# GpSimd splits the expert weights beside the experts, and second attention's units stand in another order

## The chip, the cores and the metric

The kernel runs on one core of one Trainium2 chip. Its time is the device time of one execution in microseconds (us), as the median of three runs. A core has a matmul engine (TensorE, PE in the profile; PEld is its weight load), VectorE (DVE), ScalarE (ACT), GpSimd (POOL) and SyncE (SP, which here issues DMAs). Each takes its instructions in the order written, and semaphores make one engine wait for another. Of the names in the profile bank is PSUM, and arena, arena2, arena3, work, norms and w_raw are large SBUF areas that many tiles share one after the other.

## The reference, cut to what matters

```python
x = layernorm(x + attn(x, Wq, Wkv, Wo, bo))              # 16 sequences, 16 heads of 64
x = layernorm(x + xattn(x, ctx, ctx, igate, fgate, rms)) # mLSTM with decays, 4 heads
# the expert layer, within it:
xn = (x - mu) * rsqrt(var + eps) * gamma + beta
scores, idx = top_k(softmax(xn @ Wr + br), 2)            # 8 experts, 2 per token
full_e = relu(xn @ W1[e] + b1[e]) @ W2[e] + b2[e]        # W1: 256 x 1024, W2: 1024 x 256
c = relu(b1) @ W2 + b2
x = layernorm(x + sum_k scores_k * (full[idx_k] - c[idx_k] + sum_e c_e))
```

x is 16 sequences of 128 tokens of 256 numbers, all float32. A float32 matmul is done here as three passes in a rounded format (fp32r): each operand is split into hi, its rounded value, and lo, what is left, and hi*hi, hi*lo and lo*hi are added up in PSUM. So each weight has to be split once: a cast to hi, and a subtraction for lo. The 8 experts' weights are 4096 words per partition each, 8192 when split.

## The kernel before, in words

Tokens go through attention in 8 pairs of sequences. A pair i has four steps s = 0 to 3 (two halves of the heads by two sequences); with n = 4i + s, PE does in each step the scores of step n + 1 (L762), then a list of filler units, then the transposes of the softmax weights of step n (L793), a second list of fillers, and the weighted sums of step n (L805). The lists come from `fillers(i, s)`. They hold the projections of the next steps (q, k, v; three passes each, L664 to L666), the output projection (w), and the units of second attention and the router for earlier pairs: X and C (transposes of the layernormed input and of the context, L705), G (gates, L711 and L713), S (gate rows to columns, L720), T (scores of second attention, L726), U (its weighted sums, L735), N and L (transposes and logits for the router, L741 and L747). All units but w write one of two PSUM banks in turn, and a unit waits until its bank was read. ACT copies a unit out of its bank in the same order as PE makes them (`copy_unit`), between its own work for the step: four exponentials of step n + 1, the copy of the transposed weights (L1045), four more exponentials, the copies of the second list, and the rounding of the weighted sums (L1051). DVE does the maxima (L1108), the lo parts, the scaling of the softmax weights (L1114, L1116), the layernorms, the gate sums (`gate_sums`), and the weighting of second attention (`weigh`, L1192).

The loop runs to i = 11: in steps 8 to 11 there is no first attention left, and the last pairs go through second attention and the router's norms, one short instruction waiting for another. GpSimd takes part in each pair: the mask (L565), three inverse square roots (L560, L570, L574), and the scaling for the router (L579, L582).

Between these, GpSimd splits the weights of expert i while pair i is in attention, in 16 parts of 256 words (`split_part`, L550 the cast, L552 the subtraction). SP loads each raw part, waits for the split and stores it in DRAM (`w_dram`), through two buffers (`w_pair`). After attention a whole split expert, 4 MB, is loaded back in one DMA into one of three places of `w_ring` (`load_expert`, L555), with its bias b1 (L556, in w_raw). Experts 0 to 2 are loaded in steps (8,1), (9,1) and (10,3). Then DVE works out the slots of the tokens, for which it waits for constants that GpSimd makes with iota (L620 to L629); GpSimd scatters the tokens with 32 indirect DMAs (L636); and the experts run over 40 tiles of 128 slots, in order of expert. Expert e of 3 to 7 is loaded once the last tile of expert e - 3 is done. At the end the results are gathered and normed.

The memory of `w_ring` is that of attention's weights and tiles: place 0 holds wq, wkv and wo, place 1 the q, k, v and gate tiles, place 2 arena2.

## Time and profile before

| | us |
|---|---|
| median of three runs (lowest to highest) | 920.82 (919.39 to 922.27) |
| the profiled execution | 924.46 |
| its span, from the first to the last instruction | 922.6 |

| engine | busy us | share of the span |
|---|---|---|
| PE | 710.0 | 77% |
| PEld | 600.5 | 65% |
| DVE | 441.9 | 48% |
| ACT | 331.3 | 36% |
| POOL | 307.8 | 33% |

The span in 40 equal slices, busy share in tenths:

```profile
PE   5898898888787987986553102999999999699762
...
DVE  3334444465363654647266600555555555255354
ACT  4565656656465565664121000222121212121100
POOL 3156335353645526356434174000000000000572
DMA  9756454453434534354355432117427311510242
```

Attention takes the first 18 slices or so, up to about 440 us; slices 19 to 22 are the last pairs' chains and the routing; 23 to 25 the scatter; then come the experts to about 860 us, and the gathering at the end. PEclk is the clock that TensorE was granted; 5 stands for half of the full speed.

### The profile page before, as it was taken

Reading aid. Unit: us, or ns where it says so; the run is one execution under the profiler, and the core shown is the slowest. Engines: PE = TensorE matmul, PEld = TensorE weight load, DVE = VectorE, ACT = ScalarE, POOL = GpSimd, SP = SyncE. Lnnn points to the kernel's source line nnn. Section 1 sums busy time; section 2 is a strip of 40 time slices with the busy share of each in tenths; the row PEclk is TensorE's granted clock in tenths of the full one; section 3 lists DMA queues with packets and bytes.
Section 4 is the critical chain, followed back from the end, with each engine's and each line's share of the span. In section 5 each row is a group of like instructions: output and inputs, shape, how many; then the busy total and the mean of one; then the engine's idle time right before and its main releaser. Section 6 shows DMA issues by size and latency. Waiting matters only on the chain.

```text
span 922.6 us, 14727 instructions
## 1 busy us (share of the span) xinstructions
PE 710.0 (77%) x4774; PEld 600.5 (65%) x4775; DVE 441.9 (48%) x906; ACT 331.3 (36%) x994; POOL 307.8 (33%) x416
## 2 busy tenths in 40 slices
PE   5898898888787987986553102999999999699762
PEld 4788787778676785865443001788888888588421
DVE  3334444465363654647266600555555555255354
ACT  4565656656465565664121000222121212121100
POOL 3156335353645526356434174000000000000572
PEclk9899989989798999999555555999999999899755
DMA  9756454453434534354355432117427311510242
GB/s 308 281 184 191 130 160 149 138 162 108 131 104 153 165 98 129 94 164 138 105 226 205 195 107 80 35 58 286 183 83 295 149 40 40 227 35 24 69 142 75
DMA packets 87141, 130.22 MB, mean 141 GB/s; under 512 B 9856, under 2 KB 72752, under 8 KB 86064
## 3 DMA queue, kind: packets, MB, share of 16 engines
q1 hardware_dynamic: 81664, 83.36, 28.2%
q0 software_dynamic: 5408, 46.15, 13.1%
q8 instruction: 33, 0.54, 0.3%
q14 instruction: 20, 0.16, 0.1%
q10 hardware_dynamic: 16, 0.01, 0.0%
HBM read 79.12 MB, written 50.36 MB: 140 GB/s over the span
## 4 chain that ended last, share of the span: by engine, by line
PE 43%; POOL 14%; issue 14%; DMA 14%; DVE 9%; SPq 5%; ACT 1%; POOLq 0%; DVEq 0%; ACTq 0%
PE bank L881 11%; DMA w_dram<-w_pair 8%; PE bank L852 4%; PE bank L854 4%; PE bank L853 4%; PE bank L862 3%; POOL arena L654 3%; POOL w_pair L552 3%; PE bank L664 3%; PE bank L666 2%; PE bank L665 2%; POOL w_pair L550 2%; PE bank L805 2%; DMA y_dram<-work 2%; DMA w_raw<-in_L_ffn_b_dram 2%
## 5 line engine op out<-in xcount | busy, mean ns | idle before, releaser
L550 POOL CAST w_pair<-work 128x256 fp32r<-128x256 f32 x128 | 60.8, 475 | 184.1 <-DMA w_dram<-w_pair 164.5
L881 PE MATMUL bank<-w_ring,hidT_hi 128*128 x320 | 119.7, 408 | 1.3 <-DVE hidT_lo L1403 1.3
L1071 ACT ACTIVATE hidT_hi<-bank 128x512 fp32r<-128x512 f32 x80 | 43.6, 596 | 181.5 <-PE bank L862 181.5
L552 POOL TENSOR_TENSOR w_pair<-work,w_pair 128x256 fp32r<-128x256 f32 x128 | 103.0, 805 | 10.2
L994 ACT ACTIVATE arena<-bank,negmx 128x128 f32<-128x128 f32 x256 | 90.8, 375 | 20.8 <-DVE negmx L1108 20.8
L881 PE MATMUL bank<-w_ring,hidT_lo 128*128 x320 | 83.3, 281 | 0.0
L1376 DVE TENSOR_TENSOR arena<-bank,w_raw 128x512 f32<-128x512 f32 x80 | 55.3, 692 | 49.6 <-PE bank L854 48.8
L852 PE MATMUL bank<-w_ring,xgT_hi 128*128 x160 | 68.7, 430 | 11.3 <-DMA w_raw<-in_L_ffn_b_dram 8.5
L555 POOL DMA_DIRECT2D w_ring<-w_dram x8 | 4.7, 590 | 217.4 <-PE bank L881 217.4
L881 PEld LDWEIGHTS bank<-w_ring,hidT_hi 128*128 128x128 f32 x320 | 60.1, 188 | 12.9 <-issue 1.8
L1382 DVE TENSOR_REDUCE work<-bank 128x256 f32<-128x512 f32 x40 | 27.7, 692 | 80.9 <-PE bank L881 71.2
L854 PE MATMUL bank<-w_ring,xgT_lo 128*128 x160 | 64.3, 402 | 0.0
L853 PE MATMUL bank<-w_ring,xgT_hi 128*128 x160 | 64.1, 401 | 0.0
L881 PEld LDWEIGHTS bank<-w_ring,hidT_lo 128*128 128x128 f32 x320 | 60.7, 190 | 1.9
L839 PE MATMUL bank<-ident,work 128*128 128x128 f32 x80 | 15.4, 275 | 53.8 <-DMA work<-xg_dram 53.8
L1403 DVE SCALAR_TENSOR_TENSOR hidT_lo<-bank,hidT_hi 128x512 fp32r<-128x512 f32 x80 | 51.6, 686 | 8.5 <-ACT hidT_hi L1071 8.5
L994 ACT ACTIVATION_READ_ACCUMULATOR arena<-bank,negmx 128x1 f32 x256 | 54.7, 214 | 0.0
L1065 ACT CAST xgT_hi<-bank 128x256 fp32r<-128x256 f32 x40 | 14.9, 373 | 97.3 <-issue 54.2
L839 PEld LDWEIGHTS bank<-ident,work 128*128 128x128 f32 x80 | 11.1, 140 | 59.3 <-issue 54.1
L1132 DVE TENSOR_TENSOR oT_lo<-bank,oT_hi 128x512 fp32r<-128x512 f32 x32 | 22.1, 690 | 52.8 <-ACT oT_hi L1051 52.8
L664 PE MATMUL bank<-xT_hi,wq_hi 128*128 128x256 f32 x128 | 39.7, 310 | 8.2 <-DVE wq_lo L1253 6.3
L762 PE MATMUL bank<-arena 64*128 64x128 f32 x512 | 41.9, 308 | 5.3 <-ACT arena L994 4.4
(215 smaller groups left out, 1854.2 us busy)
## 6 DMA issues: line engine op xcount, KB each, us to landing
w_dram<-w_pair SPq DMA_DIRECT2D x128, 256.0 KB, 2.3
w_ring<-w_dram POOLq DMA_DIRECT2D x8, 4096.0 KB, 12.9
work<-in_L_ffn_W_dram SPq DMA_DIRECT2D x128, 128.0 KB, 2.8
xg_dram<-work SPq DMA_DIRECT2D x10, 512.0 KB, 8.9
work<-xg_dram SPq DMA_DIRECT2D x40, 128.0 KB
y_dram<-work SPq DMA_DIRECT2D x40, 128.0 KB, 1.7
work<-gmax_dram SPq DMA_DIRECT2D x16, 256.0 KB, 3.9
w_raw<-in_L_ffn_b_dram POOLq DMA_DIRECT2D x8, 512.0 KB, 14.0
```

What stands on the lines that cost most here:

```text
L550: pool.tensor_copy(hi, raw).then_inc(w_rounded, 1)
L552: pool.tensor_tensor(lo, raw, hi.bitcast(F32), ALU.subtract).then_inc(w_split, 1)
L664: pe.matmul(out, l_hi, r_hi, start=start, stop=False)
L762: last = pe.matmul(ps_score[:, (4 * odd + h) * S:(4 * odd + h + 1) * S], qT[r:r + HD, ch, b * S:(b + 1) * S], kT[r:r + HD, ch, b * S:(b + ...
L852: pe.matmul(bank[1 + half][:, :], xgT_hi[:, par, c, :], hi, start=c == 0, stop=False)
L853: pe.matmul(bank[1 + half][:, :], xgT_hi[:, par, c, :], lo, start=False, stop=False)
L854: last = pe.matmul(bank[1 + half][:, :], xgT_lo[:, par, c, :], hi, start=False, stop=c == KC - 1)
L881: last = pe.matmul(o, l, r, start=c == 0 and l is both[0], stop=c == FC - 1 and l is both[0])
L994: last = nc.scalar.activation(probs[:, n % 2, h * S:(h + 1) * S], ps_score[:, h * S:(h + 1) * S], ACT.Exp, bias=negmx[:, n % 2, h:h + 1], ...
L1071: nc.scalar.activation(hidT_hi[:, par, 4 * half:4 * half + 4, :], bank[3 + half][:, :].rearrange("p (c t) -> p c t", c=4), ACT.Relu)\
L1376: dve.tensor_tensor(hid[par][:, half * 512:(half + 1) * 512], bank[1 + half][:, :], b1_rep[:, e % RING, half * 512:(half + 1) * 512], ALU. ...
L1403: dve.scalar_tensor_tensor(lo, bank[3 + half][:, :], 0.0, hi.bitcast(F32), ALU.max, ALU.subtract)\
```

## The change

GpSimd no longer splits in parts, and nothing goes through `w_dram`. `w_raw` now holds one expert's raw weights (b1 gets a place of its own). An expert is split in two parts of 2048 words, W1 and W2, each with one cast and one subtraction that write `w_ring` directly; right after, the same part of the next expert is loaded into `w_raw`. The first half of expert 0 is split in step (7,3), its second half in (8,1) together with the three first biases, the first half of expert 1 in (8,2), and the rest of expert 1 and all of expert 2 in (10,3), after the router's scaling of the last pair. Experts 3 to 7 are split beside the experts. PE waits for `w_split` ahead of each half of a tile.

In the fillers S, T, X, C, G and L move later; ACT's decays (four exponentials for each sequence) and gate functions move to other steps; and on DVE `weigh` and `read_gates` come after the scaling of the softmax weights, and the router's norms before the gate sums.

```diff
-            def split_part(e, k):
...
-                pool.tensor_copy(hi, raw).then_inc(w_rounded, 1)
...
-                pool.tensor_tensor(lo, raw, hi.bitcast(F32), ALU.subtract).then_inc(w_split, 1)
-
-            def load_expert(e):
-                pool.dma_start(w_ring[:, e % RING, :], w_dram[e]).then_inc(w_loaded, 16)
...
+            def load_raw(e, part):
+
+                if part == 0:
+                    pool.dma_start(w_raw[:, 0:KC * F].rearrange("p (c f) -> p c f", c=KC),
+                                   w1[e].rearrange("(c p) f -> p c f", p=P)).then_inc(w_loaded[0], 16)
+                else:
+                    pool.dma_start(w_raw[:, KC * F:].rearrange("p (c n) -> p c n", c=FC),
+                                   w2[e].rearrange("(c p) n -> p c n", p=P)).then_inc(w_loaded[1], 16)
+
+            def load_bias(e):
+                if e > 0:
+                    pool.wait_ge(b1_loaded, 16 * e)
+                pool.dma_start(b1_rep[:, e % RING, :], b1[e:e + 1, :].broadcast_to([P, F])).then_inc(b1_loaded, 16)
+
+            def split(e, part):
+
+                n = (512, D)[part]
+                half = slice(part * W_WORDS, (part + 1) * W_WORDS)
+                both = w_ring[:, e % RING, half].rearrange("p (g k n) -> p g k n", k=2, n=n)
+                raw = w_raw[:, part * KC * F:(part + 1) * KC * F].rearrange("p (g n) -> p g n", n=n)
+                pool.wait_ge(w_loaded[part], 16 * e + 16)
+                pool.tensor_copy(both[:, :, 0, :], raw).then_inc(w_rounded, 1)
+                pool.wait_ge(w_rounded, 2 * e + part + 1)
+                pool.tensor_tensor(both[:, :, 1, :], raw, both[:, :, 0, :].bitcast(F32), ALU.subtract)\
+                    .then_inc(w_split, 1)
+                if e + 1 < E:
+                    pool.wait_ge(w_split, 2 * e + part + 1)
+                    load_raw(e + 1, part)
...
-                    if i < PAIRS:
-                        for k in range(PER_STEP * s, PER_STEP * (s + 1)):
-                            split_part(i, k)
...
+                    if (i, s) == (PAIRS - 1, 2):
+                        done(pool, ("v", PAIRS - 1, 1, 1))
+                        for part in range(2):
+                            load_raw(0, part)
+                    if (i, s) == (PAIRS - 1, 3):
+                        split(0, 0)
                     if (i, s) == (PAIRS, 1):
...
-                        load_expert(0)
...
+                        for k in range(RING):
+                            load_bias(k)
+                        split(0, 1)
+                    if (i, s) == (PAIRS, 2):
+                        split(1, 0)
                     if (i, s) == (PAIRS + 2, 3):
-                        pool.wait_ge(w_loaded, 64)
-                        load_expert(2)
+                        split(1, 1)
+                        for part in range(2):
+                            split(2, part)
...
-                pool.wait_ge(w_loaded, 32 * e)
-                load_expert(e)
+                load_bias(e)
+                for part in range(2):
+                    split(e, part)
...
             if s == 0:
-                return (of("S", i - 2) + of("k", i, 2) + of("q", i, 2) + of("w", i - 1, 1, 0),
-                        of("w", i - 1, 1, 1) + of("q", i, 3) + of("k", i, 3) + of("N", i - 4))
+                return (of("k", i, 2) + of("q", i, 2) + of("w", i - 1, 1, 0),
+                        of("w", i - 1, 1, 1) + of("q", i, 3) + of("S", i - 2) + of("k", i, 3) + of("N", i - 4))
             if s == 1:
-                return (of("v", i, 1, 0) + of("T", i - 2),
-                        of("v", i, 0, 1) + of("v", i, 1, 1) + of("L", i - 4) + of("X", i - 1) + of("C", i - 1))
+                return (of("v", i, 1, 0), of("v", i, 0, 1) + of("L", i - 4) + of("v", i, 1, 1) + of("T", i - 2))
             if s == 2:
-                return (of("x", i + 1, 0) + of("x", i + 1, 1) + of("G", i - 1) + of("q", i + 1, 0) + of("k", i + 1, 0),
-                        of("q", i + 1, 1) + of("k", i + 1, 1))
+                return (of("x", i + 1, 0) + of("x", i + 1, 1) + of("X", i - 1) + of("C", i - 1)
+                        + of("q", i + 1, 0) + of("k", i + 1, 0), of("q", i + 1, 1) + of("G", i - 1) + of("k", i + 1, 1))
...
+                    if s == 1 and 0 <= i - 2 < PAIRS:
+                        decays(i - 2, 0)
+                    if s == 3 and 0 <= i - 1 < PAIRS:
+                        soft_gates(i - 1)
+                    copies(before[:split])
+                    if n + 1 < STEPS * PAIRS:
+                        exponentials(n + 1, 0)
+                    copies(before[split:])
                     if s == 1 and 0 <= i - 2 < PAIRS:
                         decays(i - 2, 1)
...
+                    if s == 3 and 0 <= i - 3 < PAIRS:
+                        both_norms(i - 3)
                     if s == 3 and 0 <= i - 1 < PAIRS:
                         gate_sums(i - 1)
-                    if s == 3 and 0 <= i - 3 < PAIRS:
-                        both_norms(i - 3)
                     if n + 1 < STEPS * PAIRS:
                         weights_of(n + 1)
+                    if s == 1 and 0 <= i - 2 < PAIRS:
+                        weigh(i - 2)
+                    if s == 2 and 0 <= i - 1 < PAIRS:
+                        read_gates(i - 1)
```

Three places of the new order follow; line numbers of the changed kernel are its own. First GpSimd in steps (8,1) to (8,3), from the mask of pair 6 (L565) and the inverse square root of pair 7 (L560) to the scaling of pair 5 for the router (L579, L582), before:

```order
L565 AFFINE_SELECT work<-work 128x512 x2
L560 TENSOR_TENSOR rstd<-ve,neghalf 128x2
L555 DMA w_ring<-w_dram 128x8192
L556 DMA w_raw<-in_L_ffn_b_dram 128x1024
L574 TENSOR_TENSOR rstd<-var,neghalf 128x4
L579 TENSOR_TENSOR arena<-arena,norms 128x512
L582 TENSOR_TENSOR arena<-arena,norms 128x512
```

And now the same stretch (L533 is the mask, L528 the square root, L547 and L550 the scaling):

```order
L533 AFFINE_SELECT work<-work 128x512 x2
L528 TENSOR_TENSOR rstd<-ve,neghalf 128x2
L509 DMA b_rep<-in_L_ffn_b_dram 128x1024 x3
L518 CAST w_ring<-w_raw 128x8x256
L520 TENSOR_TENSOR w_ring<-w_raw,w_ring 128x8x256
L503 DMA w_raw<-in_L_ffn_W_dram 128x8x256
L542 TENSOR_TENSOR rstd<-var,neghalf 128x4
L518 CAST w_ring<-w_raw 128x4x512
L520 TENSOR_TENSOR w_ring<-w_raw,w_ring 128x4x512
L500 DMA w_raw<-in_L_ffn_W_dram 128x2x1024
L547 TENSOR_TENSOR arena<-arena,norms 128x512
L550 TENSOR_TENSOR arena<-arena,norms 128x512
```

Two splits with their loads, and three biases in place of one, now stand between the square root of pair 7 and the scaling of pair 5 (L547, L550).

GpSimd at the end of the last pair's chain, from its scaling for the router to the scatter, before:

```order
L579 TENSOR_TENSOR arena<-arena,norms 128x512
L582 TENSOR_TENSOR arena<-arena,norms 128x512
L555 DMA w_ring<-w_dram 128x8192
L556 DMA w_raw<-in_L_ffn_b_dram 128x1024
L620 IOTA work 128x8
```

And now:

```order
L547 TENSOR_TENSOR arena<-arena,norms 128x512
L550 TENSOR_TENSOR arena<-arena,norms 128x512
L518 CAST w_ring<-w_raw 128x8x256
L520 TENSOR_TENSOR w_ring<-w_raw,w_ring 128x8x256
L503 DMA w_raw<-in_L_ffn_W_dram 128x8x256
L518 CAST w_ring<-w_raw 128x4x512
L520 TENSOR_TENSOR w_ring<-w_raw,w_ring 128x4x512
L500 DMA w_raw<-in_L_ffn_W_dram 128x2x1024
L518 CAST w_ring<-w_raw 128x8x256
L520 TENSOR_TENSOR w_ring<-w_raw,w_ring 128x8x256
L503 DMA w_raw<-in_L_ffn_W_dram 128x8x256
L591 IOTA work 128x8
```

Three splits with their loads come ahead of the constants that the routing needs (L591, L620 before).

ACT in step 1 of a pair in the middle of attention, from the decays (L1018) to the transposes' copies, before (L964 copies a v unit, L981 L, L968 X and C):

```order
L1018 ACTIVATE work<-work,gtok 128x128 x8
L994 ACTIVATE arena,rsum<-bank,negmx 128x128 x4
L964 COPY arena<-bank 128x512
L1045 COPY arena<-bank 128x1024
L994 ACTIVATE arena,rsum<-bank,negmx 128x128 x4
L964 COPY arena<-bank 128x512 x2
L981 COPY lg_all<-bank 128x16
L968 COPY work<-bank 128x512 x2
```

And now (L992 are the decays, L938 the v units, L955 L):

```order
L992 ACTIVATE work<-work,gtok 128x128 x4
L968 ACTIVATE arena,rsum<-bank,negmx 128x128 x4
L938 COPY arena<-bank 128x512
L992 ACTIVATE work<-work,gtok 128x128 x4
L1023 COPY arena<-bank 128x1024
L968 ACTIVATE arena,rsum<-bank,negmx 128x128 x4
L938 COPY arena<-bank 128x512
L955 COPY lg_all<-bank 128x16
L938 COPY arena<-bank 128x512
```

One half of the decays now stands between the first v copy and the copy of the transposed weights, the copy of L between those of two v units, and X and C have gone to step 2.

## Rows read from the trace of the kernel before

**Rows 1.** Windows view: columns are stretch, length, busy time per engine, PEclk, DMA share, GB/s.
```profile
87.25:415.88 328.63, 279.61 (x2335) 245.74 (x2336) 165.96 (x348) 191.69 (x634) 157.06 (x228) 0.93 0.43 135
...
415.88:457.42 41.54, 25.34 (x195) 21.89 (x194) 23.35 (x55) 14.00 (x43) 22.42 (x31) 0.79 0.38 121
457.42:505.30 47.88, 21.57 (x94) 17.49 (x95) 29.85 (x80) 9.50 (x27) 19.14 (x19) 0.50 0.53 208
```

**Rows 2.** Waits of PE, 0 to 440 us: us in total, times, longest us.
```profile
PE bank L741 <- POOL arena L582: 13.8, 4, 4.8
PE bank L720 <- ACT arena L1011: 12.2, 7, 3.9
PE bank L726 <- ACT arena L964: 11.2, 6, 2.3
PE bank L705 <- DVE xres L1155: 8.4, 7, 2.6
PE bank L711 <- DVE xT_lo L1124: 6.9, 6, 1.2
```

**Rows 3.** Timeline of PE, scores of five steps: start us, us, instruction, [idle before].
```profile
310.40 1.26 PE L762 MATMUL bank<-arena 64*128 64x128 f32 x16
...
323.02 1.16 PE L762 MATMUL bank<-arena 64*128 64x128 f32 x16
...
332.41 1.16 PE L762 MATMUL bank<-arena 64*128 64x128 f32 x16
...
350.42 1.71 PE L762 MATMUL bank<-arena 64*128 64x128 f32 x16
...
365.00 1.16 PE L762 MATMUL bank<-arena 64*128 64x128 f32 x16
```

**Rows 4.** Timeline of ACT, in the same pair.
```profile
339.13 0.37 ACT L994 ACTIVATE arena<-bank,negmx 128x128 f32<-128x128 f32 x1 [1.52 <-DVE negmx L1108]
...
360.08 0.61 ACT L964 COPY arena<-bank 128x512 f32<-128x512 f32 x1
```

**Rows 5.** Groups of POOL: busy us, mean ns, idle before.
```profile
L552 POOL TENSOR_TENSOR w_pair<-work,w_pair 128x256 fp32r<-128x256 f32 x128 | 103.0, 805 | 10.2
L550 POOL CAST w_pair<-work 128x256 fp32r<-128x256 f32 x128 | 60.8, 475 | 184.1 <-DMA w_dram<-w_pair 164.5 <-DMA work<-in_L_ffn_W_dram 19.4
...
L535 POOL TENSOR_TENSOR wo_lo<-arena,wo_hi 128x2048 fp32r<-128x2048 f32 x1 | 6.5, 6504 | 0.1
...
L533 POOL CAST wo_hi<-arena 128x2048 fp32r<-128x2048 f32 x1 | 1.9, 1889 | 14.1 <-DMA arena<-in_L_attn_Wo_dram 14.1
```

**Rows 6.** Timeline of POOL, last pairs.
```profile
443.75 0.40 POOL L550 CAST w_pair<-work 128x256 fp32r<-128x256 f32 x1 [7.88 <-DMA w_dram<-w_pair]
...
457.42 0.69 POOL L560 TENSOR_TENSOR rstd<-ve,neghalf 128x2 f32<-128x2 f32 x1 [3.88 <-DVE ve L1150]
...
481.25 0.63 POOL L565 TENSOR_SCALAR_AFFINE_SELECT work<-work 128x512 f32<-128x512 f32 x1 [0.24 <-ACT work L1018]
...
503.51 1.26 POOL L582 TENSOR_TENSOR arena<-arena,norms 128x512 f32<-128x512 f32 x1
```

**Rows 7.** Timeline of DVE: two splits at the start, last pairs, routing.
```profile
12.42 2.29 DVE L1253 TENSOR_TENSOR wkv_lo<-work,wkv_hi 128x2048 fp32r<-128x2048 f32 x1 [1.31 <-ACT wkv_hi L1027]
16.60 3.45 DVE L1253 TENSOR_TENSOR wkv_lo<-norms,wkv_hi 128x2048 fp32r<-128x2048 f32 x1 [1.89 <-ACT wkv_hi L1027]
...
453.64 1.29 DVE L1192 SCALAR_TENSOR_TENSOR work<-bank,work 128x512 f32<-128x512 f32 x2 [13.10 <-POOL work L565]
...
511.83 0.29 DVE L1315 TENSOR_TENSOR work<-work 128x128 f32<-128x128 f32 x1
```

**Rows 8.** Timeline of PE, first matmul of the last expert.
```profile
802.91 0.79 PE L852 MATMUL bank<-w_ring,xgT_hi 128*128 x1 [8.53 <-DMA w_raw<-in_L_ffn_b_dram]
```

**Rows 9.** Timeline of POOL, load of the last expert.
```profile
788.26 0.53 POOL L555 DMA_DIRECT2D w_ring<-w_dram  x1 [79.41 <-PE bank L881]
```

**Rows 10.** Page, DMA issues: KB each, us to landing.
```profile
work<-gmax_dram SPq DMA_DIRECT2D x16, 256.0 KB, 3.9
```

More of the change, by code:

```diff
@@ L101, in decoder_layer @@
         norms = sb("norms", [P, 2 * 4 * D + 2 * D])
-        CHUNK = 256
-        PARTS = W_WORDS // CHUNK
-        PER_STEP = PARTS // STEPS
-        w_pair = [over(4 * at, base, name, 2 * CHUNK)[:, :]
-                  for at, base, name in ((15360, arena_at, "w_pair0"), (6400, arena2_at, "w_pair1"))]
         hidT_lo = over(0, norms_at, "hidT_lo", 2 * F)[:, :].rearrange("p (z c t) -> p z c t", z=2, c=FC)
@@ L319, in decoder_layer @@
         scattered = sem("scattered")
-        part_loaded = [sem(f"part_loaded{k}") for k in range(4)]
-        pair_stored = [sem(f"pair_stored{k}") for k in range(2)]
-        w_loaded = sem("w_loaded")
+        w_loaded = [sem(f"w{k + 1}_loaded") for k in range(2)]
+        b1_loaded = sem("b1_loaded")
         w_rounded = sem("w_rounded")
@@ L474, in spread_maxima @@
                         .then_inc(mrep_loaded[b], 16)
-            for k in range(4):
-                load_part(0, k)
             for i in range(LAST):
@@ L599, in _ @@
                         rstd_of_pair(i - 1)
-                    if i < PAIRS:
-                        for k in range(PER_STEP * s, PER_STEP * (s + 1)):
-                            split_part(i, k)
                     if s == 2 and 0 <= i - 3 < PAIRS:
@@ L1035, in _ @@
                     before, after = fillers(i, s)
[L1036 removed]
+                    split = {0: 1, 1: 0, 2: 4, 3: 2}[s] if i < PAIRS else 0
+                    if s == 1 and 0 <= i - 2 < PAIRS:
[6 more added lines that the diff above has]
+                    copies(before[split:])
                     if s == 1 and 0 <= i - 2 < PAIRS:
                         decays(i - 2, 1)
[L1039 to L1042 removed]
                     if i < PAIRS:
@@ L1271, in _ @@
                         head_sums(i - 3)
-                    if s == 1 and 0 <= i - 2 < PAIRS:
-                        weigh(i - 2)
                     if s == 1 and 0 <= i - 1 < PAIRS:
```

61 lines of the change are left out of this document (6 added, 55 removed).

## The prediction

> **What bounds the kernel now.** I read the windows view first, to see which stretch has idle time on PE. From 87.25 to 415.88 us, six pairs of attention, PE is busy 279.61 of 328.63 us at a mean granted clock of 0.93 of full speed, so PE is the bound and 49 us are gaps [rows 1]. The next stretch, to 457.42, is 41.54 us with PE busy 25.34, and the one to 505.30 has PE busy 21.57 of 47.88 at clock 0.50: these are chains from engine to engine, in which any instruction that is put in front of a chain's next link costs its full length [rows 1].
>
> The waits of PE name the gaps. In attention five waits of second attention and the router sum to 13.8 + 12.2 + 11.2 + 8.4 + 6.9 = 52.5 us; the largest is for GpSimd's scaling L582 [rows 2]. GpSimd is late for it because its own queue stands: the casts of the weight parts (L550) waited 164.5 us in all for the store of a pair buffer, beside 163.8 us of work, 103.0 + 60.8 [rows 5]. One such wait took 7.88 us [rows 6]. So the weights' way through DRAM holds up the mask, the square roots and the scaling that stand behind it on GpSimd.
>
> The timeline of PE gives the steps of a pair, from one scores (L762) to the next: 12.6 us for step 2 (310.40 to 323.02), 9.4 for step 3, 18.0 for step 0, 14.6 for step 1 [rows 3].
>
> **The change in attention.** No split is left on GpSimd before step (7,3). The waits of rows 2 per occurrence are 3.45 (N), 1.7 (S), 1.9 (T), 1.2 (X) and 1.15 us (G), together 9.4 in a pair that has all of them [rows 2]. N's goes with the splits; the other four go because their units stand later while their makers don't. PE's work is the same.
>
> But new waits come, since units write two banks in turn and ACT frees them in order. In step 0 the unit k3 comes two after q3, and q3's copy stands behind the second four exponentials; these can't start sooner than now, since the first four waited for DVE's maximum already (1.52 us at 339.13, 6.7 after the step began) [rows 3, 4]. That puts q3's copy at about 11.8 us into the step, and PE, which arrives at 9.4 without its old waits, waits 2.4. In step 1 half of the decays now stands before the copy of the transposed weights, and L between the two v units: the second v unit needs the bank of the first, whose copy comes behind the exponentials as at 360.08 before [rows 4]; 2.7 us. In step 2 X waits for the lo part of x on DVE, 1.1 us. Together 6.2, so a late pair gains 3.2 in waits. Fewer gaps also return clock: at half clock the scores of 350.42 take 1.71 us and not 1.16 [rows 3], and some 1.5 us a pair should come back. Against 54.6 us (12.6 + 9.4 + 18.0 + 14.6) this gives 50. The early pairs have no N and L, and no split-up v units, so fewer of the new waits. Over six pairs I take 4.8 each, 29 us. Bounds: 55, if no new wait appears and all of the 49 us of gaps and 6 of clock go, and 10, if the new waits are half as long again (9.3 against 9.4, which leaves the clock). The first pair has almost none of this: 1 us.
>
> **Steps (7,2) to (8,1), 415.88 to 457.42.** GpSimd's wait of 7.88 us for a store stood ahead of the scaling, N, the decays and the mask [rows 6], and DVE sat 13.10 us until that mask was done, at 453.64, with the layernorm of pair 7 queued behind `weigh` until 457.42 [rows 7, 6]. The wait goes, and `weigh` no longer stands ahead, 1.3 us plus the handover: about 11 us. Against it the first split stands on GpSimd in (7,3), mostly beside the gate sums' round trip; I charge 3. That leaves 8 gained (4 to 12).
>
> **Price of a split.** A part is 2048 words. The trace has both forms once: cast 1.89 us, subtraction 6.50 [rows 5]. But the subtraction ran beside DVE's 128x2048 one. The 512-word L582 took 1.26 [rows 6], four times which is 5.0. I take 4.9 where DVE is idle, so 6.8 for a part, and up to 8.4 otherwise. DVE's second subtraction of that size took 3.45 us against 2.29 for the first, and it began at 16.60, under GpSimd's cast [rows 7]: two such instructions don't run side by side.
>
> The Trainium skill states it as a rule (SBUF — State Buffer, on the port pair that VectorE and GpSimd share): a VectorE instruction with two SBUF inputs, and a GpSimd one that reads SBUF, exclude each other for the whole instruction, whoever comes second. The trace agrees, by the 3.45 against 2.29 above. By that rule long GpSimd instructions are worse for DVE's chains than the 128 short ones were; this is the slower rival below.
>
> **The last pairs, 457.42 to 505.30.** Between the square root of pair 7 (457.42) and its mask (481.25) [rows 6] GpSimd now has two splits, 13.6 us; three biases in place of one, where each of two waits for the landing of the one before, some 3.5 us each, an estimate from the 3.9 us of the maxima's broadcast loads [rows 10]; and two more DMA issues, 0.5 each. GpSimd was busy only 19.14 of 47.88 us there [rows 1], so some is hidden; adding up the chain (biases to 9 us, split to 16, square root and split to 25, scaling of pair 5 to 28, N, ACT's copy and decays to 33.5) puts the mask 10 us later. DVE's norms and gate sums run beside these splits; I add 2 for the exclusion. 12 us lost (7 to 18).
>
> **Ahead of the routing.** The last scaling ended at 504.77 (503.51 + 1.26) [rows 6]. Three splits, 20.4, three loads at 0.53, 1.6, and the first iotas, 0.4, put the constants at 527.2. DVE first used them at 511.83 [rows 7]. Nothing hides this, since each token's slot hangs on it: 15 us lost (14 to 20, the upper end with 8.4 a part).
>
> **Experts.** The last expert was asked for at 788.26 [rows 9] and its first matmul came at 802.91, after PE waited 8.53 us [rows 8]. Now its raw weights lie in SBUF long before; the first half is ready 0.5 + 6.8 us after 788.3, at 795.6, so PE, idle from 794.4, waits 1.2. That is 7.3 gained, and about 1 of clock, since behind the wait that matmul took 0.79 us [rows 8]; the bias, 0.5 MB with an empty queue, lands before. Second half: 802.5, before the tile needs it. Splits of experts 3 to 6 have an expert's time each and more. DVE there reads one operand from PSUM. I take 8.5 (3 to 10).
>
> **The sum.** -29 - 1 - 8 + 12 + 15 - 8.5 = -19.5 us. The profiled execution's 924.46 would become 905.0. The median of the runs is 920.82, 3.6 less, which I take as the same for both kernels: 901.3, so 901.
>
> **Rivals.**
> PE-bound attention: the new bank waits don't come, since ACT's copies are quicker than I have them. For it: ACT was busy only 191.69 of 328.63 us [rows 1]. Against: its order, not its load, makes the wait. It gains 46 to 55 in place of 29, so -37 to -46: about 880.
> Attention's gain is small: the new order costs on PE what GpSimd's freedom gives (12 to 18 gained). For it: T, X and G meet two banks in new turns. Around 914.
> Slower, by the port pair: GpSimd's casts and subtractions of 2 to 5 us hold off DVE's two-input instructions and scalings in (7,3) to (8,3), each for the rest of a GpSimd instruction, so that pair 7's gates come 10 us later than charged, and the splits take 8.4 (+5 in the routing). That is 901 + 10 + 5 = 916; it decides from the point where attention gives under 24 us in place of 29. With attention at 14 it is 916 + 15 = 931. Against it: there are only three splits in that stretch, and the chains before were mostly waiting.
> The change doesn't do what it says: an expert's tiles wait for its split. For it: the subtraction could take longer beside DVE. Each expert but the last has over 20 us for it; on the last it turns -8.5 into -3. It is inside the range.
>
> **How the numbers follow.** Forecast, 0.57 (its own range 891 to 911). PE-bound, 0.18. Small gain, 0.15. Slower, 0.10. No change is what a measurement can't tell from it, 0.3% or 2.8 us: 918.1 to 923.6. Faster: 0.57 + 0.18 + 0.11 of the small gain = 0.86; same: 0.05, from the small gain's upper end and a weaker slower case; slower: 0.09. The range reaches to 882, leaving the best of PE-bound out, and to 917.
>
> **What would show it.** The steps from scores to scores in a pair in the middle: about 15, 12.5, 13.5 and 9 us for steps 0 to 3, with PE's waits for second attention's units replaced by waits of 2 to 3 us for ACT's copies of a q and a v unit. GpSimd with three pairs of cast and subtraction, 1.9 and about 4.9 us, between the last scaling and the iotas, and DVE waiting some 15 us for them. A wait of about 1 us ahead of the last expert. Wrong: a pair under 47 or over 53 us, or a stretch from pair 7's square root to its mask under 30 or over 42 us.

## The result, and the profile after

| us | before | after |
|---|---|---|
| median (lowest to highest) | 920.28 (919.16 to 922.27, 8 runs) | 927.59 (924.62 to 932.62, 8 runs) |
| span of the profiled execution | 922.6 | 925.2 |

The ratio of after to before is 1.0083, with a 95% interval of 1.0057 to 1.011: the changed kernel is slower by 0.8%, where 901 was forecast. The windows view of after, cut at the same events as before (square root of pair 0, of pair 6, of pair 7; mask of pair 7; end of the last scaling; first scatter; gathering); columns as in [rows 1]:

```profile
83.50:397.87 314.37, 273.40 (x2320) 240.00 (x2318) 165.18 (x346) 187.74 (x634) 34.60 (x36) 0.95 0.07 20
397.87:440.04 42.17, 25.24 (x202) 21.40 (x204) 28.74 (x55) 16.19 (x54) 16.30 (x13) 0.79 0.29 95
440.04:477.79 37.75, 12.93 (x64) 9.41 (x62) 20.74 (x38) 7.25 (x21) 22.66 (x17) 0.55 0.33 111
477.79:502.80 25.01, 8.66 (x44) 7.80 (x44) 16.67 (x44) 1.98 (x6) 9.56 (x9) 0.50 0.00 0
502.80:541.61 38.81, 4.15 (x16) 3.42 (x16) 22.24 (x57) 1.38 (x4) 22.72 (x17) 0.50 0.25 81
541.61:866.89 325.28, 275.14 (x1544) 232.97 (x1544) 147.86 (x240) 60.52 (x124) 105.64 (x66) 0.92 0.24 79
```

Before, the square root of pair 0 was at 86.49, that of pair 6 at 415.15 and the last scaling's end at 504.77. [rows 1] are cut 0.7 us later, at 415.88, so that the stretches of before are these:

```profile
86.49:415.15 328.66, 278.88 (x2329) 245.01 (x2329) 165.96 (x348) 191.87 (x636) 157.06 (x229) 0.93 0.43 135
415.15:457.42 42.27, 26.07 (x200) 22.62 (x200) 23.35 (x55) 14.58 (x44) 23.15 (x32) 0.80 0.37 119
457.42:481.25 23.83, 12.87 (x56) 9.39 (x56) 13.19 (x36) 7.24 (x20) 7.94 (x9) 0.50 0.57 221
...
504.77:526.25 21.48, 4.16 (x16) 3.43 (x16) 14.30 (x57) 1.38 (x4) 2.14 (x9) 0.50 0.55 220
526.25:860.89 334.64, 278.06 (x1544) 235.18 (x1544) 147.81 (x240) 60.55 (x124) 36.20 (x42) 0.91 0.31 115
```

| | forecast | measured |
|---|---|---|
| to the square root of pair 0 | -1 | 83.50 - 86.49 = -3.0 |
| six pairs | -29 | 314.37 - 328.66 = -14.3 |
| steps (7,2) to (8,1) | -8 | 42.17 - 42.27 = -0.1 |
| last pairs | +12 | 62.76 - 47.35 = +15.4 (+13.9 up to the mask) |
| ahead of the routing's scatter | +15 | 38.81 - 21.48 = +17.3 |
| scatter and experts | -8.5 | 325.28 - 334.64 = -9.4 |
| the end (before 860.89 to 922.6, after 866.89 to 925.2) | 0 | 58.3 - 61.7 = -3.4 |

These add up to +2.5, and the spans differ by 2.6. The medians differ by 7.3, since before's profiled execution was 4.2 above its median and after's 0.7 below. So the costs of the change were forecast 6 us too low in sum, and attention's gains 20 us too high. One profile is not exact for attention: experiments 4 and 6, which have after's instructions up to pair 6's square root, took 320.9 us for the six pairs, 6.5 more than after's profile. So 8 to 14 of the forecast 29 us came.

PE's waits of after, 0 to 440 us (columns as in [rows 2], to which they answer):

```profile
PE bank L636 <- ACT arena L938: 10.9, 4, 2.8
PE bank L636 <- DVE oT_lo L1106: 10.4, 1, 10.4
PE bank L636 <- ACT arena L934: 9.7, 6, 2.3
PE bank L698 <- ACT arena L938: 8.6, 6, 2.8
```

The waits for GpSimd's scaling (N), for the exponential of the gates (S, L1011) and of G in [rows 2] are gone. In their place stand the second v unit (L636 for the copy L938), k3 (L636 for L934) and X (L677 for the lo part of x, 7.2 us in six), as forecast, T as before, and one wait of 10.4 us in step (8,0). The timeline of PE in a pair in the middle answers to [rows 3]; L734 is the scores, x1 stands for one matmul and the bracket for the idle time ahead of it:

```profile
278.28 1.41 PE L734 MATMUL bank<-arena 64*128 64x128 f32 x16
...
286.99 0.80 PE L636 MATMUL bank<-wkv_hi,xT_hi 128*128 128x512 f32 x1 [2.66 <-ACT arena L938]
...
294.60 1.77 PE L734 MATMUL bank<-arena 64*128 64x128 f32 x16
...
309.21 1.16 PE L734 MATMUL bank<-arena 64*128 64x128 f32 x16
...
318.60 1.16 PE L734 MATMUL bank<-arena 64*128 64x128 f32 x16
...
325.55 1.09 PE L765 MATMUL bank<-ident,arena 128*128 128x128 f32 x8 [1.27 <-DVE arena L1090]
...
332.11 0.38 PE L636 MATMUL bank<-xT_hi,wkv_hi 128*128 128x256 f32 x1 [2.26 <-ACT arena L934]
...
336.67 1.24 PE L734 MATMUL bank<-arena 64*128 64x128 f32 x16
```

The waits are of the size that was forecast, 2.66 for 2.7 and 2.26 for 2.4. But step 1 (from 278.28) took 16.3 us for 12.5, step 2 14.6 for 13.5, step 0 18.1 for 15, and behind the wait of 2.66 the scores took 1.77 and not 1.16. The granted clock fell while PE stood idle in that wait, and from its end to 296.30 it was 0.52, the lower of its two levels but for the end of the stretch:

```profile
286.99:296.30 9.31, 8.54 (x55) 6.79 (x55) 2.94 (x4) 1.20 (x3) 0.00 (x0) 0.52 0.01 2
```

After that it was 1.00, and again 0.51 for the 3.3 us from 333.39, behind the wait of 2.26. The prediction named a pair over 53 us as a sign of being wrong, and the late pairs took 57.3, 58.3 and 54.8.

GpSimd in the last pairs and ahead of the routing:

```profile
460.08 4.50 POOL L520 TENSOR_TENSOR w_ring<-w_raw,w_ring 128x2048 fp32r<-128x2048 f32 x1
...
467.01 1.26 POOL L550 TENSOR_TENSOR arena<-arena,norms 128x512 f32<-128x512 f32 x1
...
502.75 1.89 POOL L518 CAST w_ring<-w_raw 128x2048 fp32r<-128x2048 f32 x1
```

A split is 1.89 + 4.50 us, for 6.8 forecast; with 0.30 of waiting for its own end and the load's issue of 0.7 to 1.0, three of them fill 502.75 to 525.7. The 6.50 us of [rows 5] were 4.50 and a hold: DVE's subtraction of 16.60 ended at 20.05, 2.06 us after that one had begun at 17.99. DVE waits for the constants meanwhile; two of its instructions there:

```profile
513.54 3.58 DVE L1283 TENSOR_TENSOR work<-work 128x128 f32<-128x128 f32 x1
526.55 0.28 DVE L1287 TENSOR_REDUCE score<-work 128x16 f32<-128x128 f32 x1 [9.43 <-POOL work L595]
```

The last expert now waits 1.26 us (forecast 1.2), where it was 8.53 [rows 8]:

```profile
811.55 0.49 PE L825 MATMUL bank<-w_ring,xgT_hi 128*128 x1 [1.26 <-POOL w_ring L520]
```

### The profile page after: what moved, and what is told of

The parts are those of the page before. It is cut to its first block, busy times and chain, and to the rows that moved or that the text cites. A ratio compares the mean times of both kernels' runs of the same rounds, so it can differ in the third digit from the quotient of the medians.

```text
span 925.2 us, 14249 instructions
## 1 busy us (share of the span) xinstructions
PE 697.9 (75%) x4774; PEld 589.4 (64%) x4775; DVE 462.3 (50%) x906; ACT 326.3 (35%) x994; POOL 258.0 (28%) x200
## 4 chain that ended last, share of the span: by engine, by line
PE 53%; DVE 13%; POOL 12%; ACT 11%; issue 6%; DMA 4%; POOLq 0%; SPq 0%; ACTq 0%; DVEq 0%
PE bank L855 12%; PE bank L636 5%; ACT arena L968 5%; PE bank L638 4%; PE bank L637 4%; PE bank L825 4%; PE bank L827 4%; PE bank L826 4%; PE bank L835 4%; POOL arena L626 3%; POOL xg_dram L607 3%; PE bank L777 3%; DVE negmx L1082 3%; POOL w_ring L520 2%; PE bank L734 2%
## 5 line engine op out<-in xcount | busy, mean ns | idle before, releaser
L1045 ACT ACTIVATE hidT_hi<-bank 128x512 fp32r<-128x512 f32 x80 | 43.5, 596 | 172.4 <-PE bank L835 172.4
L968 ACT ACTIVATE arena<-bank,negmx 128x128 f32<-128x128 f32 x256 | 91.5, 383 | 22.2 <-DVE negmx L1082 22.2
L1350 DVE TENSOR_TENSOR arena<-bank,b_rep 128x512 f32<-128x512 f32 x80 | 55.3, 692 | 41.9 <-PE bank L827 41.6
L520 POOL TENSOR_TENSOR w_ring<-w_raw,w_ring 128x2048 fp32r<-128x2048 f32 x16 | 72.9, 4557 | 1.3
L855 PEld LDWEIGHTS bank<-w_ring,hidT_hi 128*128 128x128 f32 x320 | 60.1, 188 | 12.6 <-issue 1.6
L968 ACT ACTIVATION_READ_ACCUMULATOR arena<-bank,negmx 128x1 f32 x256 | 56.7, 221 | 0.0
L509 POOL DMA_DIRECT2D b_rep<-in_L_ffn_b_dram x8 | 4.5, 563 | 165.0 <-PE bank L855 158.0
L811 PEld LDWEIGHTS bank<-ident,work 128*128 128x128 f32 x80 | 11.2, 141 | 59.6 <-issue 54.4
L636 PE MATMUL bank<-xT_hi,wkv_hi 128*128 128x256 f32 x128 | 39.7, 310 | 10.7 <-ACT arena L934 9.7
L636 PE MATMUL bank<-wo_hi,oT_hi 128*128 128x256 f32 x128 | 38.7, 302 | 10.4 <-DVE oT_lo L1106 10.4
L636 PE MATMUL bank<-xT_hi,wq_hi 128*128 128x256 f32 x128 | 38.8, 303 | 9.2 <-DVE wq_lo L1227 5.9
L734 PE MATMUL bank<-arena 64*128 64x128 f32 x512 | 39.8, 298 | 6.2 <-ACT arena L968 4.7
## 6 DMA issues: line engine op xcount, KB each, us to landing
xres<-in_x_dram SPq DMA_DIRECT2D x1, 2048.0 KB, 15.4
```

The costliest lines, as they stand in the source:

```text
L520: pool.tensor_tensor(both[:, :, 1, :], raw, both[:, :, 0, :].bitcast(F32), ALU.subtract)\
L636: pe.matmul(out, l_hi, r_hi, start=start, stop=False)
L734: last = pe.matmul(ps_score[:, (4 * odd + h) * S:(4 * odd + h + 1) * S], qT[r:r + HD, ch, b * S:(b + 1) * S], kT[r:r + HD, ch, b * S:(b + ...
L855: last = pe.matmul(o, l, r, start=c == 0 and l is both[0], stop=c == FC - 1 and l is both[0])
L968: last = nc.scalar.activation(probs[:, n % 2, h * S:(h + 1) * S], ps_score[:, h * S:(h + 1) * S], ACT.Exp, bias=negmx[:, n % 2, h:h + 1], ...
L1045: nc.scalar.activation(hidT_hi[:, par, 4 * half:4 * half + 4, :], bank[3 + half][:, :].rearrange("p (c t) -> p c t", c=4), ACT.Relu)\
```

## Experiments

All are edits of the changed kernel, "after" below, unless it says otherwise. Medians are compared with its 927.59; ratios, with 95% intervals, are to the kernel before, timed on the same chip.

**1. GpSimd's part alone.** The fillers and the loops of ACT and DVE stand in the old order.

```diff
-                return (of("v", i, 1, 0), of("v", i, 0, 1) + of("L", i - 4) + of("v", i, 1, 1) + of("T", i - 2))
+                return (of("v", i, 1, 0) + of("T", i - 2),
+                        of("v", i, 0, 1) + of("v", i, 1, 1) + of("L", i - 4) + of("X", i - 1) + of("C", i - 1))
...
```

> GpSimd's new way of splitting, with the units, ACT and DVE in the order of the kernel before. Theory A (the new order of units costs in the late pairs what GpSimd's freedom gives): the waits for the scaling go, none of the new bank waits comes, so pairs 4 to 6 take 50 to 53 us each in place of 54.8 to 58.3, and the time is 908 to 920. Theory B (the late pairs are bound by something that neither touches, so order is neutral): pairs 4 to 6 stay at 54 to 58, the early pairs lose what the new order gave them, and the time is 925 to 938.

908.68 us (906.02 to 911.21), ratio 0.9856 (0.9821 to 0.9891), 18.9 less than after, as by Theory A. A late pair took 51.3 us at clock 0.97, for 54.8 to 58.3 in after.

**2. The new order alone**, on the kernel before.

> The splits in parts through DRAM as before, with the new order of units alone. Theory A: pairs 4 to 6 at 56 to 60 us, early pairs a little quicker, no cost in the last pairs and the routing; the time is within 10 us of the kernel before, 912 to 930. Theory B: the time falls by the 17 us that attention gained in the changed kernel, to 903 to 908.

923.0 us (919.61 to 927.97), ratio 1.0016 (0.9992 to 1.0039). Its first pair period (square root to square root) fell from 51.9 to 47.6, its fourth rose from 58.4 to 61.1. So the order by itself is worth nothing here (the interval includes 1), and with GpSimd free (1) it costs 19 us.

**3. The router's norms on DVE behind the gate sums again.**

```diff
-                    if s == 3 and 0 <= i - 3 < PAIRS:
-                        both_norms(i - 3)
                     if s == 3 and 0 <= i - 1 < PAIRS:
                         gate_sums(i - 1)
+                    if s == 3 and 0 <= i - 3 < PAIRS:
+                        both_norms(i - 3)
```

> The changed kernel with DVE's norms for the router put back behind the gate sums in step 3 (two lines swapped). Theory A: the second pair of norms and the first gate instruction no longer meet GpSimd's scaling (they took 1.69 and 1.32 us in place of 0.73 and 0.33), and the gate sums end 3.6 us earlier in a step 3, so the wait for the scaled softmax weights (5.1 us in all) and 2 us per late pair go: 8 to 12 us, 916 to 920. Theory B: nothing waits for these, within 2 us of the changed kernel.

921.19 us (915.85 to 925.43), ratio 1.0001 (0.9973 to 1.0029). This is between the two theories, and what Theory A gave to the late pairs didn't come: the three took 170.3 us as in after. The 6.4 us come from where splits stand: steps (7,2) to (8,1) took 36.3 us for 42.2, and pair 7's square root to its mask 33.2 for 37.75, 10.4 less together, while the six pairs took 2.8 more in this profile. In after DVE in (7,3) shows, with GpSimd beside it:

```profile
421.30 6.57 DVE L1150 TENSOR_TENSOR_SCAN arena<-arena 4x128 f32<-4x128 f32 x2
```

```profile
421.08 1.95 POOL L518 CAST w_ring<-w_raw 128x2048 fp32r<-128x2048 f32 x1
423.10 4.50 POOL L520 TENSOR_TENSOR w_ring<-w_raw,w_ring 128x2048 fp32r<-128x2048 f32 x1
```

And in this experiment, ahead of GpSimd's split at 425.07, with PE's wait in (8,0):

```profile
419.11 0.73 DVE L1150 TENSOR_TENSOR_SCAN arena<-arena 4x128 f32<-4x128 f32 x2
```

```profile
PE bank L636 <- DVE oT_lo L1106: 3.6, 1, 3.6
```

The two scans of the gate sums take 0.73 us when free. In after they came 0.2 us behind the start of the cast and ended 0.3 us behind the subtraction; the lo parts that PE needs are queued behind them, and PE's wait was 10.4 us for 3.6. In (8,2) the gate sums still met a split in this experiment (a subtraction of 4 x 256, L1158, took 4.54 us for 0.41), but that cost little, since GpSimd's own queue was full until 461.57 and its scaling stood 0.18 us behind that.

**4. The three splits of (10,3) behind the scatter's issues.**

```diff
-                    if (i, s) == (PAIRS + 2, 3):
-                        split(1, 1)
-                        for part in range(2):
-                            split(2, part)
...
+            split(1, 1)
+            for part in range(2):
+                split(2, part)
+
             for e in range(RING, E):
```

> The changed kernel with the three splits of step (10,3) put behind the scatter's issues. Theory A: the constants come as soon as before, the routing starts 17 to 22 us earlier, and the splits (20 us) end before expert 1 starts: 905 to 911. Rival: the splits show up again, as a wait of PE for expert 1 or as slower scatter DMAs, and less than 10 us is left: 918 to 925.

914.94 us (911.21 to 916.38), ratio 0.993 (0.9903 to 0.9956), 12.7 less, and 4 above Theory A's range. From the last scaling to the first scatter 21.6 us for 38.8, and from there to the gathering 325.5 for 325.3: all 17.2 us of the stretch come back, and the experts don't miss the splits. The median moved 4 less. Attention took 5 us longer in this profiled execution, with the same instructions: over the six pairs PE's work took 280.4 us for 273.4, more of it at half clock. Why is not shown.

**5. S behind k3, and L behind both v units**, so that q3 and k3, and the two v units, are neighbours in the two banks.

```diff
-                        of("w", i - 1, 1, 1) + of("q", i, 3) + of("S", i - 2) + of("k", i, 3) + of("N", i - 4))
+                        of("w", i - 1, 1, 1) + of("q", i, 3) + of("k", i, 3) + of("S", i - 2) + of("N", i - 4))
...
-                return (of("v", i, 1, 0), of("v", i, 0, 1) + of("L", i - 4) + of("v", i, 1, 1) + of("T", i - 2))
+                return (of("v", i, 1, 0), of("v", i, 0, 1) + of("v", i, 1, 1) + of("L", i - 4) + of("T", i - 2))
```

> The changed kernel with two units moved in the filler lists: S behind k3 in step 0, L behind both v units in step 1, so that k3 and the second v unit write the bank freed before the second four exponentials. Theory A (these two waits, 2.3 and 2.7 us, and the half clock that follows them make the late pairs 57 us): both waits shrink or pass to the short units, PEclk goes from 0.88-0.91 to 0.95 or more, pairs 4 to 6 take 52 to 54, and the time is 910 to 917 against the changed kernel's 924 to 928. Theory B (the wait only moves to the next unit and nothing is won): within 4 us of the changed kernel.

913.18 us (909.18 to 917.49), ratio 0.9938 (0.9906 to 0.997), 14.4 less. The waits for a bank didn't go: they passed to the short units. The 2.3 us ahead of k3 became 1.1 ahead of S, and the 2.7 ahead of the second v unit became 2.2 ahead of L (L719), four times:

```profile
PE bank L719 <- ACT arena L938: 8.8, 4, 2.2
```

**6. Memsets in place of the first three splits**: those parts of the weights are zeros here, so that GpSimd is about as long at it (7.3 us for 6.5) but reads nothing from SBUF.

```diff
+                if 2 * e + part < 3:
+                    pool.memset(both[:, :, 0, :].bitcast(F32), 0.0).then_inc(w_rounded, 1)
+                    pool.memset(both[:, :, 1, :].bitcast(F32), 0.0).then_inc(w_filled, 1)
...
```

> In the changed kernel the first three splits, in (7,3), (8,1) and (8,2), are replaced by four memsets of 2048 words each, about as long, which read nothing; the experts 0 and 1 then compute with zeros in these parts. Theory A (GpSimd's instructions that read SBUF hold off DVE's two-input instructions): the scan that took 6.57 us for two takes 0.7 to 2, PE's wait of 10.4 us for the lo part behind it goes to 4 or less, and the time is 5 to 9 us below the changed kernel's, though GpSimd's queue is as full. Theory B (only the place in GpSimd's queue costs): the scan is still slow or the time is within 2 us.

928.79 us (926.27 to 931.42), ratio 1.0104 (1.006 to 1.0148): no gain in the time. DVE in (7,3), and GpSimd beside it:

```profile
426.15 4.78 DVE L1158 TENSOR_SCALAR arena<-arena,fb 4x256 f32<-4x256 f32 x1
430.96 0.73 DVE L1161 TENSOR_TENSOR_SCAN arena<-arena 4x128 f32<-4x128 f32 x2
...
461.65 5.31 DVE L1224 TENSOR_SCALAR arena<-xres,mv,rboth 128x256 f32<-128x256 f32 x2
```

```profile
426.04 1.26 POOL L561 TENSOR_TENSOR arena<-arena,norms 128x512 f32<-128x512 f32 x1
...
428.99 1.80 POOL L521 MEMSET w_ring<- 128x2048 f32 x1
430.84 1.83 POOL L523 MEMSET w_ring<- 128x2048 f32 x1
```

The scans now run beside a memset in 0.73 us, but the scaling ahead of them (L1158), 0.33 us when free, was held by GpSimd's own scaling (L561) and then to the end of the second memset. In after it took 1.30 us (L1147), so the two together were held for 4.5 us here and 6.8 in after. PE's wait in (8,0) was 8.1 us for 10.4, where Theory A had 4 or less, and steps (7,2) to (8,1) took 38.1 us for 42.2. That is lost again: 1.6 us up to pair 7's mask, as each replacement is 0.8 us longer than a split, and 6.5 over the six pairs, which the edit doesn't touch. So part of the price of the split of (7,3) is the hold and not GpSimd's queue, but this run doesn't separate the two by the time of the kernel.

**7. GpSimd's part alone (1) with the splits behind the scatter (4).**

> GpSimd's new way of splitting with the old order of units, and the three splits of (10,3) behind the scatter's issues. If the effects of these two add up, 908.7 less 12.6 (from 927.6 to 914.9): 896 (892 to 900). If the early constants only expose another wait of the routing in the old order: over 902.

889.48 us (887.71 to 890.48), ratio 0.9684 (0.965 to 0.9718), 19.2 less than (1) and below the expected range. The stretch ahead of the scatter gained 17.1 us on (1), as in (4), and not the 12.6 by which the median had moved there.

**8. As 7, but experts 0 to 2 are split during the scatter by ACT (cast) and DVE (subtraction)**, from raw weights that SP loads, so that GpSimd has no split before the scatter's issues.

```diff
+            act.wait_ge(route_ready, 1)
+            for e in range(RING):
+                for part in range(2):
+                    both, raw = halves(e, part)
+                    act.wait_ge(w_fetched[part], 16 * e + 16)
+                    nc.scalar.copy(both[:, :, 0, :], raw).then_inc(w_rounded, 1)
...
```

> Old order of units; experts 0 to 2 are split by ACT (cast) and DVE (subtraction) while GpSimd issues the scatter, with raw loads and biases by SP; GpSimd splits only experts 3 to 7. Theory A (GpSimd's six splits cost by its queue and by holding off DVE, and nothing else bounds these stretches): from the mask of pair 7 on as in the kernel before, 427.5 less the 2 of the first split, plus 47.4 and 21.5 us, gives 495 for the first scatter and 395 us from there as in the kernel before less 8: 880 (875 to 888). Rival: the loads and DVE's reads slow the scatter, or expert 0 waits: over 890.

885.91 us (884.61 to 886.77), ratio 0.9637 (0.9602 to 0.9671), the fastest of all. The square root of pair 7 and its mask, and the first scatter:

```profile
418.31 0.69 POOL L562 TENSOR_TENSOR rstd<-ve,neghalf 128x2 f32<-128x2 f32 x1 [3.88 <-DVE ve L1147]
...
442.09 0.63 POOL L567 TENSOR_SCALAR_AFFINE_SELECT work<-work 128x512 f32<-128x512 f32 x1 [0.25 <-ACT work L1009]
...
487.07 1.23 POOL L625 DMA_INDIRECT xg_dram<-arena,slot  x1 [16.23 <-DVE slot L1368]
```

From square root to mask it is 23.78 us, as in before (23.83), for 36.4 in (7): two splits and three biases on GpSimd cost 12.6 us there, and the split of (7,3) 3.2 more. But from the first scatter to the gathering it took 338.2 us for 324.9, so 13.3 of the 15.8 went again: the scatter's 32 issues took 47.5 us (487.07 to 534.57) for 39.5 in (7), and PE waited 5.0 us for the last expert for 1.3 in (7), as its split waited 3.80 us for the landing of its bias. One of GpSimd's issues, and DVE beside it:

```profile
503.14 2.54 POOL L625 DMA_INDIRECT xg_dram<-arena,slot  x1 [0.30 <-issue]
```
```profile
502.55 2.29 DVE L1392 TENSOR_TENSOR w_ring<-w_raw,w_ring 128x2048 fp32r<-128x2048 f32 x1 [1.82 <-ACT w_ring L1073]
```

An issue that begins under a subtraction ends 0.8 us after it and takes 2.54 us, the others 0.96. There are six subtractions and six issues of 1.90 to 2.64 us, together 8.0 us above 0.96: the whole loss of the scatter. The six were those that began under a subtraction; issues beside ACT's casts alone took 0.96.

**9 and 10. Each move of (5) alone**: S behind k3 (9), L behind the v units (10).

> The changed kernel with one of the two moves of the bank experiment: only S stands behind k3, so k3 no longer waits for q3's copy; L stays between the two v units. Theory A (the waits for a bank cost their own length and, each for itself, a share of the clock): PE's wait ahead of k3 (2.3 us a pair) goes, the wait of the second v unit (2.8) stays, a late pair takes 54 to 55 us in place of 57 to 58, and the kernel some 920 us against 927.6. Theory B (the clock falls as long as either wait is left): a late pair gains no more than the 2.3 us, the clock stays at 0.88 to 0.91, 922 to 925 us. Rival: S, now later, comes late for its own chain on ACT and DVE, and the decays of step 1 with it: no gain.

> The changed kernel with the other move: only L stands behind both v units, S stays ahead of k3. Theory A: the second v unit's wait (2.8 us) goes, k3's (2.3) stays; a late pair takes 54 to 55 us, the kernel some 920 us. Theory B: 922 to 925 us, clock 0.88 to 0.91. In both, the gains of this kernel and of the one with S alone would have to add up to the 14.4 us of the two moves together if waits cost each for itself, and fall well short of it by Theory B.

9: 922.78 us (921.29 to 924.53), ratio 1.0028 (1.0013 to 1.0042), 4.8 less. 10: 928.55 us (922.92 to 929.4), ratio 1.0075 (1.005 to 1.0099), 1.0 more. Both moves together gave 14.4, and the two alone 3.8 in sum, which by the second expectation speaks for Theory B. The eight times of (10) are in two groups, 922.9 to 923.7 and 928.4 to 929.4, and its profile is of the fastest, so its periods are better than its median. The period from the square root of pair 4 to that of pair 5, in before, after, 5, 9, 10, 1 and 11 (all three mended, below), in this order:

```profile
304.76:360.83 56.07, 47.66 (x397) 41.73 (x397) 30.06 (x65) 32.50 (x108) 27.67 (x39) 0.94 0.42 132
```
```profile
284.82:343.08 58.26, 49.82 (x396) 43.39 (x396) 30.48 (x65) 31.70 (x108) 7.25 (x8) 0.88 0.07 19
```
```profile
281.60:332.83 51.23, 44.65 (x396) 39.28 (x396) 30.41 (x65) 31.66 (x108) 7.25 (x8) 1.00 0.07 22
```
```profile
282.42:337.26 54.84, 47.39 (x396) 41.35 (x396) 30.50 (x65) 31.66 (x108) 7.26 (x9) 0.94 0.07 20
```
```profile
281.57:336.63 55.06, 47.54 (x396) 41.91 (x396) 30.50 (x65) 31.60 (x108) 7.26 (x8) 0.94 0.08 21
```
```profile
287.23:338.57 51.34, 45.58 (x397) 40.53 (x397) 30.33 (x65) 31.94 (x108) 7.32 (x7) 0.97 0.07 22
```
```profile
279.95:333.75 53.80, 47.48 (x396) 41.84 (x396) 30.34 (x65) 31.83 (x108) 7.29 (x9) 0.94 0.07 21
```

The second number less the third is PE's idle time: 8.4, 8.4, 6.6, 7.5, 7.5, 5.8 and 6.3 us. The third is the time of the same 396 matmuls (397 in two of the rows), and it follows the granted clock: 49.8 us at 0.88, 47.4 to 47.7 at 0.94, 45.6 at 0.97, 44.7 at 1.00. Of the 7.0 us between after and (5), 1.9 is idle time and 5.2 is clock. In this period each move alone gives half, clock included, as Theory A has it; from pair 0's square root to pair 7's they give 3.3 and 3.0 us and both together 17.9, as Theory B has it. Neither theory holds in full.

Nor is the clock settled by the waits that are left. (5) and (11) have both moves and the same waits in this period, 2.2 us ahead of L among them. In (5) the clock stayed at 1.00 through it, in this period and the next; in (11) it was 0.50 for the 6.2 us behind it, and the matmuls took 47.5 us. What is shown is that after a wait of 2 to 3 us the clock can be halved for longer than the wait, and that this took more of the time between after and (5) than the waits did. What decides whether it is halved, and what the norms' order has to do with it in (11), no run shows.

**11. All of 3, 4 and 5.**

> The changed kernel with all three of its own parts mended: both bank moves, the router's norms on DVE back behind the gate sums, and the three splits of step (10,3) behind the scatter's issues. Each alone gave -14.4, -6.4 and -12.7 us. If they lie in different stretches they add up: 927.6 - 33.5 = 894 us (889 to 899). Rival: the norms' gain (the gates of pair 7 no longer under the split) and the bank moves' gain are in part the same time, 900 to 904 us. A late pair should take 51 to 52 us at a clock of 0.97, pair 7's square root come by 421 us, and the scatter start about 29 us after the last scaling's end less the three splits, 21 to 22 us.

890.34 us (889.4 to 892.21), ratio 0.9674 (0.9653 to 0.9695), 37.3 less than after; 33.5 was the sum of the three. The time is in the expected range, but its late pairs are not: 52.5, 53.8 and 53.9 us for 51 to 52, at clock 0.97 and 0.94, and pair 7's square root came at 424.45 and not by 421. So the change's splits can stand in its new order too, but that gives nothing over the old order (889.48 in 7).

## Why the prediction was wrong

The sign was wrong. Taken by its steps:

**Attention, -29: failed, -14.3.** The step that failed is "a late pair gains 3.2 in waits" and "some 1.5 us a pair should come back" of clock. The early pairs gained more than 4.8 each (51.9 to 43.5, 52.1 to 47.5), at a clock of 1.00 for 0.90 and 0.94. The late ones gained nothing: 58.4, 56.1 and 54.3 us became 57.3, 58.3 and 54.8. PE's idle time in these three fell by 0.4 us a pair, and its work took 0.9 us a pair more, at clocks of 0.91, 0.88 and 0.97 for 0.91, 0.94 and 0.97. The three new waits came with their sizes (2.7, 2.3 and 1.1 in the fifth period, for 6.2 in sum), but two that the sum had at nothing stood beside them: T's for L938 (0.8 there, 8.6 in all, for 11.2 before), and one for DVE in step 0 (1.3). And the old idle time was smaller than 9.4 in the fifth and sixth periods, 8.4 and 8.3. On the clock, the mistake was to give the new waits none of their own while giving the removed ones 1.5 us. Experiment 5 shows what the order of S and L costs: with both moved, that period takes 51.2 us. Experiment 1 shows that the gain was there: GpSimd's freedom with the old order takes the six periods in 304.8 us, 23.9 less than before; the new order gives 9.6 of these back.

**Steps (7,2) to (8,1), -8: failed, -0.1.** "Mostly beside the gate sums' round trip; I charge 3" is the step. It was the gate sums themselves that met the split, held for 5.8 us (6.57 for 0.73), because the diff puts the router's norms ahead of them on DVE. The price of that order is 5.9 us in this stretch (experiment 3). With it mended the stretch is 36.3, 6.0 less than before, within the bounds (4 to 12).

The Trainium skill's rule, quoted in the prediction (SBUF — State Buffer, on the port pair of VectorE and GpSimd), was the ground of the slower rival, and the trace bears it out: scans with two SBUF inputs waited for cast and subtraction, and didn't wait for memsets. The rival's +10 in (7,3) to (8,3) is about what came: these stretches cost 7.9 and 3.4 us more than forecast, and experiment 3 takes 5.9 + 4.5 back by DVE's order. How much of that is the hold and how much GpSimd's queue is in part argued, since experiment 6 gave 4.1 back in the first stretch and nothing in the second. None of its +5 in the routing came, as no split took 8.4 us.

**Last pairs, +12: too low, +15.4.** GpSimd's chain came as added up, biases to 9.3 us behind the square root, first split to 15.8, the scaling to 28.2 (28). From there to the mask it took 9.5 us and not 5.5, again by the norms ahead of the gates: with experiment 3's order it is 33.2 in all for the forecast 33.5.

**Ahead of the routing, +15: too low, +17.3.** The mechanism was right and two sizes were off. A split was cheaper than taken (6.4 for 6.8), but 0.30 us of waiting stands behind each subtraction and an issue took 0.7 to 1.0 us for 0.53. And DVE's wait is at 526.55, ahead of L1287, which is L1313 in before, there at 511.18 and so two instructions before the one that the sum took as the first user [rows 7]. From the last scaling's end to that instruction it is 23.75 us for 6.41, and the difference is the 17.3. DVE's instructions there were held by the splits too (3.58 us for 0.29), but that lies under the wait.

**Experts, -8.5: right, -9.4**, with the wait ahead of the last one as forecast. The end gave 3.4 more, which the sum had at nothing. It is not all chance: the end took 58.1 to 58.4 us in every profile in which GpSimd loads the raw weights, and 61.7, 59.9 and 59.7 in before, (2) and (8), where SP loads all or some of them. 2.3 us of it lie behind the issue of the last store (5.6 us to the end in before, 3.3 in after). Why is open. By the medians the change is worse than by the two profiles.

The forecast was the one of four cases in which both gains of attention come; the small gain (12 to 18 forecast, 8 to 14 measured) was what happened there, and the slower rival's mechanism was on top of it. Either alone had been priced at 914 and 916; both together at 931. The range left out their coincidence, though one diff made both.

## What to carry to other kernels

A wait of 2 to 3 us on TensorE inside a stretch at full clock should be charged with the half-clock time that can follow it, as a range: that was the larger part here (5.2 us beside 1.9 in one period), but the same wait of 2.2 us cost no clock in one run and was followed by 6.2 us at half clock in another. What a long instruction on GpSimd costs depends on what VectorE has queued at that moment, and not only on whether GpSimd is free: a pair of scans of 0.73 us took 6.57. And where a diff makes one engine free and reorders the others as well, each half should be summed alone: here GpSimd's half was worth 12 us on the kernel before, 31 with three splits placed late, and the new order nothing or less.

## What the runs showed of the hardware

- GpSimd memsets of 1.8 us, which read nothing, held VectorE scalings with one SBUF input: one of 4 x 256 took 4.78 us (0.33 when free), under a GpSimd instruction of 1.26 us and then two memsets, and a pair of 128 x 256 took 5.31 us (0.73 when free, as in 3), over three memsets. Scans with two inputs ran beside a memset in 0.73 us (experiment 6), and took 6.57 us beside cast and subtraction (after).
- The clock's price is visible in one kind of row: the same 396 matmuls took 44.65 us at a mean granted clock of 1.00 and 49.82 at 0.88. Behind the same idle time of 2.2 us it was 1.00 in experiment 5 and 0.50 in 11.
- A VectorE subtraction with two SBUF inputs held the issue of GpSimd's indirect DMAs: 1.90 to 2.64 us for 0.96, once for each of six (experiment 8).

The Trainium skill (SBUF — State Buffer, on the two separate sides) has the first: a VectorE instruction in a mode that uses both port pairs, and one with two SBUF inputs against a GpSimd instruction that reads SBUF, lock out the other engine. It counts the scaling's form among those that can enter such a mode. That a memset holds the scaling and not the scan agrees, if the scaling ran in such a mode, which no row tells. For the third it names the lock on writing DMA descriptors for the two-port mode alone, and says that an instruction with two SBUF inputs did not stall DMAs; here one did, by experiment 8, for indirect DMAs.
